# A fused adaLN block with test-time-training attention and routed experts: the steps of each engine in another order

## What is computed

```
mod = silu(c) @ wmod -> sa, ca, ga, sb, cb, gb       # scale, shift and gate rows
h = layernorm(x) * (1 + ca) + sa
q, k, v = silu(h @ W_qkv); q, k = q / |q|, k / |k|   # 4 heads of 128
lr0, lr1, lr2 = softplus(h @ W_lr + b)               # 3 rates per head and token
for each chunk of 128 tokens (16 chunks, w0, w1, w2 carried on):
    gate = k @ w0; hb = k @ w2; sg = silu(gate); hidden = sg * hb
    dhidden = v @ w1.T
    w1 += ns(hidden * lr1, v);  w0 += ns(k * lr0, silu'(gate) * dhidden * hb)
    w2 += ns(k * lr2, dhidden * sg)
    each w rescaled to its old column norms
    o = silu(q @ w0) * (q @ w2) @ w1                 # w after the update
x = x + ga * (rmsnorm(o) @ W_proj)
h2 = layernorm(x) * (1 + cb) + sb
top 2 of 8 experts by softmax(h2 @ (gate_w + lora)); each expert a silu-gated
    MLP 512 -> 256 -> 512 whose weights have low-rank (LoRA) additions
x = x + gb * (weighted sum of the two experts)
```

## Time and profile before

| | |
|---|---|
| median of 3 runs | 1005.18 us (1003.49 to 1005.67) |
| profiled execution | 1002.81 us, span 1001.1 us, mean granted clock 0.959 |
| busy, share of the span | PE 88%, PEld 53%, DVE 66%, ACT 65%, POOL 35% |
| PE busy | 881.9 us in 5127 matmuls |
| from the first chunk's norm product to the last one's | 90.83 to 658.79 us |
| period in the middle of it | 40.27 us |
| chain that ended last | PE 59%, DVE 16%, DMA 7%, POOL 7%, issue 6%, ACT 4% |

### The profile page before, as it was taken

One profiled execution on the slowest core, in us unless ns is written; L12 is line 12 of the kernel. 1 busy time (PEld: TensorE's weight loads), 2 busy tenths in 40 slices (PEclk: granted clock), 3 DMA queues, 4 the chain that ended last, 5 costly groups with the idle time before them and its releaser, 6 DMA issues.

```text
span 1001.1 us, 16358 instructions
## 1 busy us (share of the span) xinstructions
PE 881.9 (88%) x5127; PEld 532.6 (53%) x5127; DVE 661.0 (66%) x2299; ACT 647.9 (65%) x1416; POOL 349.8 (35%) x285
## 2 busy tenths in 40 slices
PE   7798998999999989999899999987469999999995
PEld 3456566565665765656657656464124444444442
DVE  3688989889889898898898887976322222222221
ACT  2767888888888888898888888874023333333331
POOL 2223344453454444534444434422102222222222
PEclk8999999999999999999999999977679999999998
DMA  9755327244153261442633513382524444443430
GB/s 334 252 149 159 107 85 191 57 134 147 56 180 106 87 191 47 145 131 71 180 88 104 159 44 106 96 341 96 214 74 85 76 77 83 75 78 73 84 48 0
DMA packets 59092, 120.43 MB, mean 120 GB/s; under 512 B 6896, under 2 KB 8560, under 8 KB 57984
## 3 DMA queue, kind: packets, MB, share of 16 engines
q1 hardware_dynamic: 50688, 102.28, 33.2%
q0 software_dynamic: 8176, 16.85, 9.0%
q10 hardware_dynamic: 144, 0.26, 0.1%
HBM read 51.94 MB, written 69.27 MB: 121 GB/s over the span
## 4 chain that ended last, share of the span: by engine, by line
PE 59%; DVE 16%; DMA 7%; POOL 7%; issue 6%; ACT 4%; SPq 0%; POOLq 0%; DVEq 0%; ACTq 0%
PE bank L714 15%; PE bank L110 11%; PE bank L116 8%; PE bank L727 7%; DMA xs_scratch<-t_arena 5%; POOL xs_scratch L1814 2%; POOL t_small L1801 2%; PE bank L487 1%; PE bank L549 1%; PE bank L498 1%; PE bank L559 1%; PE bank L503 1%; PE bank L529 1%; PE bank L467 1%; PE bank L536 1%
## 5 line engine op out<-in xcount | busy, mean ns | idle before, releaser
L110 PEld LDWEIGHTS bank<-t_arena 128*128 128x128 bf16 (+1 forms) x1536 | 123.5, 122 | 83.6 <-issue 15.9
L714 PE MATMUL bank<-t_arena 128*128 x312 | 145.9, 611 | 19.0 <-issue 17.5
L110 PE MATMUL bank<-t_arena 128*128 128x128 bf16 (+1 forms) x1536 | 152.7, 236 | 8.7 <-DVE t_arena L860 2.3
L116 PE MATMUL bank<-t_ident,t_arena 128*128 128x128 f32 x618 | 102.6, 285 | 41.5 <-DMA t_arena<-xs_scratch 8.4
L1840 POOL DMA_INDIRECT out_x<-t_arena,t_tokx x39 | 60.6, 1553 | 208.6 <-DVE t_small L1367 197.2
L116 PEld LDWEIGHTS bank<-t_ident,t_arena 128*128 128x128 f32 x618 | 72.4, 143 | 98.7 <-issue 40.4
L1372 DVE TENSOR_TENSOR t_arena<-t_arena,bank 128x256 f32<-128x256 f32 x39 | 16.4, 421 | 144.9 <-ACT t_arena L1722 144.9
L1722 ACT ACTIVATE t_arena<-bank 128x256 f32<-128x256 f32 x39 | 15.0, 384 | 148.7 <-PE bank L714 148.7
L714 PEld LDWEIGHTS bank<-t_arena 128*128 128x128 f32 x312 | 56.7, 192 | 85.3 <-issue 85.3
L727 PE MATMUL bank<-t_arena 128*128 x156 | 73.5, 593 | 0.5 <-ACT t_arena L1717 0.5
L1729 ACT ACTIVATE t_arena<-bank,t_small 128x128 f32<-128x128 f32 x156 | 58.7, 456 | 15.7 <-PE bank L116 13.7
(11 more groups left out here) (510 smaller groups left out, 2189.3 us busy)
## 6 DMA issues: line engine op xcount, KB each, us to landing
xs_scratch<-t_arena SPq DMA_DIRECT2D x16, 2064.0 KB, 11.6
wm_scratch<-t_arena SPq DMA_DIRECT2D x48, 256.0 KB, 2.3
t_arena<-wm_scratch SPq DMA_DIRECT2D x8, 1536.0 KB, 12.4
t_arena<-xs_scratch SPq DMA_DIRECT2D x39, 258.0 KB, 2.7
t_arena<-in_gate_up SPq DMA_DIRECT2D x32, 256.0 KB, 3.6
t_arena<-in_wmod SPq DMA_DIRECT2D x6, 1024.0 KB, 11.3
t_arena<-in_down SPq DMA_DIRECT2D x16, 256.0 KB, 3.6
out_x<-t_arena SPq DMA_DIRECT2D x16, 256.0 KB, 2.0
```

Of the source, the lines that this page charges most:

```text
L110: mm = pe.matmul(bank[:, s], lhs[:, s], rhs[:, s], start=True, stop=True)
L116: mm = pe.transpose(bank[:, 128 * k:128 * k + 128], src[:, 128 * k:128 * k + 128], idn)
L714: mm = pe.matmul(AA[u % 2][:, :], xT[u % 2][:, 128 * k:128 * k + 128], w_e[:, bass.ds(which[u], 1), 512 * k:512 * k + 512], start=(k == 0) ...
```

## The change

The operations, their shapes and the SyncE list are the same. The lists of TensorE, VectorE, ScalarE and GpSimd are written in another order, in the setup, in the loop and a little just behind it, with the tables and waits to match. The diff is some 1,500 lines of moved steps; its core, with the tables first:

```diff
-PREP_DVE = ("bnst", "bnag", "ve", "hA", "n8", "n8e", "r8", "tk", "tq")
+PREP_DVE = ("bnst", "bnag", "ve", "hA", "n8", "n8e", "r8", "tq", "tk")
-PREP_ACT = ("hT", "raw0", "raw1", "sq", "raw2", "kT", "vT", "qT", "kl0", "vl", "kl2")
+PREP_ACT = ("hT", "raw1", "raw0", "sq", "raw2", "qT", "vT", "kT", "vl", "kl0", "kl2")
-MG_DVE = ("u1", "u2", "u0")
+MG_DVE = ("u0", "u2", "u1")
...
                 if p < NC:
-                    pe.wait_ge(prep_dve, nth(PREP_DVE, p, "tk"))
-                    pe.wait_ge(prep_act, nth(PREP_ACT, p, "raw1"))
-                    turned(pe, P1, raw[1], 4, ident[:, :]).then_inc(prep_pe, 1)
+                    pe.wait_ge(prep_dve, nth(PREP_DVE, p, "tq"))
+                    pe.wait_ge(prep_act, nth(PREP_ACT, p, "raw2"))
+                    turned(pe, P0, raw[0], 4, ident[:, :]).then_inc(prep_pe, 1)
+                    turned(pe, P2, raw[2], 4, ident[:, :]).then_inc(prep_pe, 1)
                 if a >= 0:
                     pe.wait_ge(apply_act, nth(APPLY_ACT, a, "lgT"))
                     pe.matmul(A0[:, 0:NE], lgT[:, :], selr[:, 0:NE], start=True, stop=True).then_inc(apply_pe, 1)
                 if p < NC:
-                    pe.wait_ge(prep_act, nth(PREP_ACT, p, "raw2"))
-                    turned(pe, P2, raw[2], 4, ident[:, :]).then_inc(prep_pe, 1)
-                    pe.wait_ge(prep_dve, nth(PREP_DVE, p, "tq"))
-                    turned(pe, P0, raw[0], 4, ident[:, :]).then_inc(prep_pe, 1)
+                    pe.wait_ge(prep_dve, nth(PREP_DVE, p, "tk"))
+                    turned(pe, P1, raw[1], 4, ident[:, :]).then_inc(prep_pe, 1)
...
                     pool.wait_ge(s_z[a % 2],16 * (a // 2 + 1))
                     pool.wait_ge(apply_dve, nth(APPLY_DVE, a, "pu"))
-                    pool.wait_ge(apply_dve, nth(APPLY_DVE, a, "dw"))
-                    pool.wait_ge(apply_dve, nth(APPLY_DVE, a, "e0"))
                     for k in range(2):
```

More of the change, by code:

```diff
@@ L304, in _ @@
             p = 0
+            pe.wait_ge(s_wm[1],16)
+            pe.wait_ge(set_dve, nth(SET_DVE, 0, "cb32"))
+            for j in range(4):
+                q = slice(32 * j, 32 * j + 32)
+                mm = pe.matmul(A0[q, :], cb32[:, q], wm[1][:, 512 * j:512 * j + 512], start=True, stop=True)
+            mm.then_inc(set_pe, 1)
             if p < NC:
```

820 lines of the change are left out of this document (410 added, 410 removed).

## The result

The changed kernel takes 1009.68 us (median of 20 runs, 1005.31 to 1013.34) against 1003.13 before (20 runs, 994.99 to 1006.25): ratio 1.0066, 95% interval 1.0051 to 1.0081. It is **slower** by 0.66%, 22 us over the forecast and outside the range. Its profiled execution took 1010.71 us, 7.9 more than that of before. The norm products of branch 2 divide it into three parts: up to the first chunk's (90.29 against 90.83) it is 0.5 shorter, from there to the last one's (669.65, so 579.36 against 567.96) 11.4 longer, and behind it (span 1009.0, so 339.35 against 342.31) 3.0 shorter.

What follows compares the result with a forecast made beforehand. TensorE was taken as the bound, with 2.70 us idle per 40.27 us period. Gains of 1.15 per period over 14 periods (16.1) plus 1.5 in setup, 17.6 in total, gave 987.6 us, range 979 to 1004.

Steps and rivals of the forecast that it cites:

- Step 1: Last Newton-Schulz polynomial: TensorE gets its inputs at 21.8 us and not 21.32 after the output product, 0.5 late.
- Step 2: Normalised k and q on VectorE: the last done at 27.08 and not 27.73, gain 0.65 us per period.
- second rival: bfloat16 adds also hold up GpSimd's square root; VectorE waits 0.9 us ahead of k; 1000 us, 12%.
- Step 3: Adapter products to the forward product with v: 4.76 us and not 4.83, gain 0.1 per period.
- Step 4: Forward product to next output product: 5.69 us and not 6.12, from earlier 1/std and gate product; gain 0.4.
- The slower rival: VectorE is held at the addition ending branch 2 by a late copy; 9 us lost, 1014 us, 17%.
- Setup: Before the loop: q, v and k copied sooner by a new transpose order, gain 1.5 us, bounds 0 and 3.

Runs made afterwards that it cites:

- e11: The changed kernel with one dummy one-input float32 sum (0.60 us) on VectorE between the two bfloat16 additions and the float32 updates: 985.60 us, ratio 0.9831.
- e1: The changed kernel with VectorE's step that waits for GpSimd's root for w2 moved behind q, k and the last sum: 976.38 us, ratio 0.9766.
- e5: The changed kernel with one dummy TensorE product of 384 columns per period ahead of the transposes of k: 991.42 us, ratio 0.9880.
- e8: e1 with the sum for branch 2's norm put back ahead of the gate product, as in the kernel before: 979.55 us, ratio 0.9766.

## Why the prediction was wrong

Two rows of the kernel before, VectorE's additions at the start of GpSimd's power at 314.19, bear on the second point:

```profile
314.03 0.42 DVE L1098 TENSOR_TENSOR t_arena<-t_arena 128x512 bf16<-128x512 bf16 x1
314.36 0.42 DVE L1100 TENSOR_TENSOR t_arena<-t_arena 128x512 bf16<-128x512 bf16 x1
```

- **Step 1 held.** The 0.5 late at the last polynomial is there (0.49, and 21.85 against 21.8).
- **Step 2 failed**, in its last sentence: "The release of 0.31 us supposes that the square root no longer lasts 1.99 us". It lasts 3.26. I let "float32 steps hold it up and bfloat16 ones not" on the row at 314.19, a power of one column that took 0.67 beside three additions. It started 0.16 into the first of them (314.03) and ended, at 314.86, 0.50 behind that one's end. The power at 330.60 likewise ended 0.52 behind the end of the float32 step beside it (330.50 and 0.60). So the row I took for a free power shows one held to the end of a bfloat16 addition, with only 0.17 left of it, and let go by the next; such a power takes 0.58 where no step with two SBUF inputs runs at its start (373.69 above). The root has four columns, and e11 shows it held by two additions to their end. The second rival had this mechanism and its numbers: through adds, updates and q until 25.7, done at 26.6 (26.58), 0.9 of wait. It got 12%. The Trainium skill, page "SBUF — State Buffer", section "Who interferes with whom", has it that a VectorE instruction with two SBUF inputs contends with a GpSimd instruction that reads SBUF, and makes no exception for a type. It was the better guide: e11 (1.46 us) agrees with it, and so does the row at 314.19, read as above, which the forecast had against it. By my own rule, too, I should have asked more: the root had 0.51 us before the first float32 update and needed 1.0.
- **The clock was priced at nothing, and it was the larger half.** The forecast said that it could not tell how many periods fall and put 1.6 to 1.9 us for each of two in the range. The runs show 1.18 in each of eleven, and more in the last three. 14 x 0.95 for the root is 13.3 and 14 x 1.18 for the clock 16.5; together 29.8 of the 34.4 us between the loops of e1 (544.93) and of the changed kernel (579.36). Most of the rest lies in the last three periods. What the forecast missed is that the two are one: a wait of 0.9 makes the gap before k 0.79 and not nothing, and the gap brings the clock down. Without the fall the second rival's period, 40.02, would have been near the 39.78 of e5, which has the root's wait and no fall; its 1000 would still have been 9 too high.
- **Step 3 held** once the clock stayed: 4.76 to the digit. **Step 4 held** in its size, 5.67 against 5.69; of its two causes the exchange carries 0.10 (e8), and the share of the earlier 1/std is not shown.
- **The slower rival did not come.** Branch 2's copy ends at 353.95 (17.57, forecast 17.6), VectorE is there at 354.15 (17.77, forecast 17.8) and waits for nothing. The kernel is slower, as this rival alone had it, but for a reason that no rival had: the root and the clock in a chain. The right sign by it would have been luck.
- **Setup and end.** Setup gained 0.5 and not 1.5. The last chunk, left as it was in the forecast, gained 3.0, all of it before the first expert block (68.22 from the last norm product to its transposes against 71.33). TensorE is busy there for 23.8 of the first 31.2 us, with no next chunk's projections to do, so that shorter chains of the new order could show in full; no run undoes that part, and the cause is not shown.
- Without the two, the forecast of the order itself was close, with a gain a little too small: a period of 39.12 against 38.83.

## What to carry to other kernels

When an order is laid out from the durations in a trace, a duration that depends on what another engine does at that moment (here GpSimd's power beside VectorE's wide steps, 1.0 to 3.26 us for one shape) is not a number to plan with: put the step that waits for it late, where its longest form does no harm. One line moved for that reason gained 0.8% on the kernel before and 3% on the changed one. And price a stall on TensorE's path twice, once for its length and once for the clock; a cheap product in the gap tells in one run whether the second price is being paid.
